# Moving one transpose per sequence from behind the scores to the end of the step before, and the first keys' copy to ScalarE, in a one-layer language-model kernel

## The reference

```python
h = layernorm(word_emb[x] + pos_emb + type_emb[mask]) * gamma + beta
a = layernorm(h)
k, q, v = a @ Wk, a @ Wq, a @ Wv              # split into 16 heads of 16
k, q = layernorm(k) * kln_w + kln_b, layernorm(q) * qln_w + qln_b   # per head
attn = softmax(causal(q @ k.T / 4))
h = h + (attn @ v) @ Wo + bo
n = layernorm(h)
scores = softmax(n @ gate_w.T);  top 2 of scores + expert_bias
h = h + sum over the two of  (silu(s*n @ w1[e]) * (s*n @ w3[e])) @ w2[e]    # s: the token's score
```

## Time and profile before

| | |
|---|---|
| Median of 3 runs | 545.32 us (545.27 to 545.44) |
| The profiled execution's own time | 545.62 us |
| Its span, first to last instruction | 543.8 us |
| Granted TensorE clock, mean | 0.992 |
| Start, 0 to 31.2 us (before the first scores): PE / DVE / ACT / POOL busy | 21.2 / 16.3 / 3.9 / 18.1 us |
| Scores of step 0 to scores of step 14, 31.2 to 186.2 us | 141.2 / 136.4 / 131.3 / 111.3 us of 155.0 |
| Last steps and routing, 186.2 to 228.8 us | 36.3 / 34.3 / 19.9 / 22.4 us of 42.6 |
| Experts, 228.8 to 543.8 us | 302.6 / 104.9 / 95.7 / 134.4 us of 315.0 |

### The profile page before, as it was taken

One profiled execution on the slowest core, in us unless ns is written; L12 is line 12 of the kernel. 1 busy time (PEld: TensorE's weight loads), 2 busy tenths in 40 slices (PEclk: granted clock), 3 DMA queues, 4 the chain that ended last, 5 costly groups with the idle time before them and its releaser, 6 DMA issues.

```text
span 543.8 us, 13452 instructions
## 1 busy us (share of the span) xinstructions
PE 501.2 (92%) x4470; PEld 428.7 (79%) x4471; DVE 291.9 (54%) x759; ACT 250.7 (46%) x575; POOL 286.2 (53%) x532
## 2 busy tenths in 40 slices
PE   5877989998999888999999999999999999999991
PEld 2345666777776665499999999999999999999980
DVE  2778888889989887733333333333333333333330
ACT  1166788978997883243223322332233323332320
POOL 4678787677764675214543454345434454344432
PEclk9999999999999999999999999999999999999996
DMA  5007721101028672302212221122112221222221
GB/s 174 10 22 243 231 85 31 58 29 29 29 80 278 212 251 84 90 22 41 29 30 39 39 39 22 37 39 39 23 36 39 39 28 31 39 38 30 30 39 19
DMA packets 29962, 36.75 MB, mean 68 GB/s; under 512 B 8272, under 2 KB 23504, under 8 KB 29936
## 3 DMA queue, kind: packets, MB, share of 16 engines
q0 software_dynamic: 8352, 12.76, 13.8%
q1 hardware_dynamic: 20768, 22.61, 13.1%
q10 hardware_dynamic: 816, 1.06, 0.6%
HBM read 26.81 MB, written 9.50 MB: 67 GB/s over the span
## 4 chain that ended last, share of the span: by engine, by line
PE 79%; DVE 5%; POOL 5%; ACT 4%; issue 3%; DMA 2%; POOLq 0%; DVEq 0%; ACTq 0%
PE PS L1445 35%; PE PS L1456 18%; PE PS L1172 10%; PE PS L1296 5%; PE PS L1254 2%; PE PS L1395 2%; PE PS L1271 2%; DMA x_pair<-word_dram,idx 1%; PE PS L1180 1%; ACT work L628 1%; PE PS L1310 1%; PE PS L1243 1%; DVE nmax L879 1%; DMA out_dram<-x_pair,dst_c 1%; POOL arena L477 1%
## 5 line engine op out<-in xcount | busy, mean ns | idle before, releaser
L1445 PEld LDWEIGHTS PS<-work,arena 128*128 128x128 f32 x1716 | 197.6, 192 | 2.3 <-ACT work L744 0.4
L1445 PE MATMUL PS<-work,arena 128*128 128x128 f32 x1716 | 198.0, 275 | 0.0
L750 ACT ACTIVATE work<-PS 128x768 f32<-128x768 f32 x39 | 31.6, 810 | 197.2 <-PE PS L1445 197.2
L1456 PE MATMUL PS<-w_sb,work 128*128 x468 | 107.6, 379 | 0.7 <-DVE x_pair L1147 0.7
L1139 DVE TENSOR_TENSOR work<-work,PS 128x640 f32<-128x640 f32 x39 | 32.0, 821 | 138.0 <-ACT work L750 138.0
L1456 PEld LDWEIGHTS PS<-w_sb,work 128*128 128x128 f32 x468 | 85.9, 190 | 11.2 <-issue 1.1
L572 POOL DMA_INDIRECT out_dram<-x_pair,dst_c x39 | 79.2, 2030 | 21.9 <-POOL dst_c L571 20.5
L571 POOL COPY dst_c<-dest_i 128x1 int32 (+1 forms) x39 | 7.1, 183 | 138.7 <-DVE x_pair L1147 136.5
L628 ACT ACTIVATE work<-PS,nmax 128x128 f32<-128x128 f32 x256 | 72.0, 401 | 3.7 <-DVE nmax L879 3.7
L740 ACT ACTIVATE arena<-w_sb 128x1408 f32 x40 | 55.1, 1379 | 12.0 <-DVE er_i L1115 9.0
L1172 PE MATMUL PS<-ident,work 128*128 128x128 f32 x336 | 54.8, 276 | 1.8 <-ACT work L628 1.8
(11 more groups left out here) (172 smaller groups left out, 618.8 us busy)
## 6 DMA issues: line engine op xcount, KB each, us to landing
w_sb<-w_dram SPq DMA_DIRECT2D x16, 640.0 KB, 5.6
w_sb<-w_dram SPq DMA_DIRECT2D x8, 704.0 KB, 4.5
x_rows<-x SPq DMA_DIRECT2D x16, 128.0 KB, 2.3
out_dram<-arena SPq DMA_DIRECT2D x16, 128.0 KB, 2.4
w_sb<-w_dram SPq DMA_DIRECT2D x16, 64.0 KB, 6.2
w_sb<-w_qkv_dram ACTq DMA_DIRECT2D x1, 768.0 KB, 8.2
work<-x_rows,src_c POOLq DMA_INDIRECT x41, 2.8
out_dram<-x_pair,dst_c POOLq DMA_INDIRECT x39
```

Of the source, the lines that this page charges most:

```text
L1445: last = n.matmul(up_ps[p][:, i, c, :], ws[p][:, k, at:at + P], xT_sb[p][:, k, :], start=(k == 0), stop=(k == DK - 1))
L1456: last = n.matmul(PS[:, 7, 0:D], hT_sb[p][:, i, :], w2_sb[:, bass.ds(e, 1), i, :], start=(i == 0), stop=(i == FK - 1))
```

## The change

Three things are edited.

- `early_rows(u)` is true for the sequences 0 to 3. For these the transposes of `a_n` stay where they were. For sequences 4 to 15 they move from step u-2, behind the scores, to the end of step u-3, behind `mask_banks`, and go to the upper half of `VY_BANK`; they wait for `a_ready`, `aT_ready` and `v_ready`. ScalarE's copy moves likewise, from the head of its step to the end of the step before.
- `outputs` waits for `aT_ready` only in step 1; from step 2 on it waits for `var_f` instead. `rank(0)`, which uses the same half of `VY_BANK`, gets a wait for the last `aT_ready`.
- The keys of sequences 0, 1 and 2 are copied out by ScalarE, at the head of `queries_out`, which for these waits for the transposes (`qk_ps`) and not for `k_ready`; the three `keys_out` calls on VectorE go. In step 0 `queries_out(1)` moves ahead of `transposed(2)`.

```diff
+        KEYS_BY_ACT = 3
+        def early_rows(u):
+            return isinstance(u, int) and u < 4
...
                 def queries_out(u):
-                    act.wait_ge(k_ready, u + 1)
+                    if isinstance(u, int) and u < KEYS_BY_ACT:
+                        act.wait_ge(qk_ps, u + 1)
+                    else:
+                        act.wait_ge(k_ready, u + 1)
                     if not isinstance(u, int) or u > 0:
                         act.wait_ge(s_done, RG * u)
+                    if isinstance(u, int) and u < KEYS_BY_ACT:
+                        a.activation(kT.rearrange("p b s -> p (b s)"), PS[:, T_BANK, D:2 * D], ACT.Identity,
+                                     scale=cols_sb[:, 4:5], bias=cols_sb[:, 5:6]).then_inc(k_ready, 1)
...
                 u = t + 2
-                if valid(u):
+                if valid(u) and early_rows(u):
                     act.wait_ge(aT_ps, u + 1)
                     wait(act, v_done, u - 1)
                     a.activation(aT[p].rearrange("p k s -> p (k s)"), PS[:, O_BANK, 0:D],
...
                     transposed(1)
+                    queries_out(1)
                     transposed(2)
-                    queries_out(1)
...
                 if valid(t):
                     transposed(3)
+                u = t + 3
+                if valid(u) and valid(t) and not early_rows(u):
+                    act.wait_ge(aT_ps, u + 1)
+                    act.wait_ge(v_done, u - 1)
+                    a.activation(aT[1 - p].rearrange("p k s -> p (k s)"), PS[:, VY_BANK, D:2 * D],
+                                 ACT.Copy).then_inc(aT_ready, 1)
...
                     normalize_a(2)
-                    keys_out(0)
...
                     first_norm(3)
-                    keys_out(1)
...
                     first_norm(4)
-                    keys_out(2)
...
                     pe.wait_ge(v_ready, B - 2)
+                    pe.wait_ge(aT_ready, B)
...
                     pe.wait_ge(v_ready, u + 1)
-                    wait(pe, aT_ready, u + 4)
+                    if at_step(t, 1):
+                        pe.wait_ge(aT_ready, u + 4)
                     if at_step(t, B):
                         pe.wait_ge(added, 1)
-                    elif edge and t + 2 >= B:
+                    else:
                         wait(pe, var_f, u)
...
                 u = t + 2
-                if valid(u):
+                if valid(u) and early_rows(u):
                     pe.wait_ge(a_ready, u + 1)
-                    wait(pe, var_f, u - 3)
                     wait(pe, aT_ready, u)
                     transposes(a_n, DK, O_BANK).then_inc(aT_ps, 1)
...
                 if valid(t + 1) and valid(t):
                     mask_banks(t + 1)
+                u = t + 3
+                if valid(u) and not early_rows(u):
+                    pe.wait_ge(a_ready, u + 1)
+                    pe.wait_ge(aT_ready, u)
+                    pe.wait_ge(v_ready, u - 1)
+                    transposes(a_n, DK, VY_BANK, D).then_inc(aT_ps, 1)
```

## The result

The changed kernel takes 547.12 us (median of 8 runs, 546.73 to 550.44), the kernel before in the same measurements 545.50 (8 runs, 545.27 to 546.01). The ratio is 1.0038, 95% interval 1.0022 to 1.0055: slower by 0.4%, 1.6 us. The forecast was slower by 1.25 us, 546.6.

The account below looks back on a forecast made before the run. TensorE, busy 501.2 of 543.8 us, was taken as the bound. Keys -1.85, moved pairs +4.18 and outputs -1.08 sum to +1.25 us on the 545.32 median: 546.6 us, range 544.3 to 548.4.

Parts of the forecast that it names:

- The wait moves to the qkn transposes: Steps 2 to 13: TensorE's wait before the outputs reappears before the qkn transposes; steps 4 to 13 gain only 1.08 us.
- Pairs of transposes in the solid row, 0.38 each: Ends of steps 1 to 12: each moved transpose pair costs TensorE 0.38 us before the next scores, 11 x 0.38 = +4.18.
- One pair free behind step 2: End of step 2: the moved pair costs nothing, as TensorE waits 0.82 us at step 3's x2 transposes anyway.
- The keys part, -1.85: Steps -1 to 1: key copies on ScalarE start squared sums, maxima and GpSimd's chain 1.85 us earlier; bounds 1.0 and 2.1.
- B: Moved pairs cost 0.22 us each, overlapped with the mask banks: sum -0.51, 544.8 us, no difference; chance 0.15.
- C: The 0.60 us wait is really saved in 12 steps, as VectorE's chain to qkn shortens: 536.1 us; chance 0.08.
- D: Step ends: the moved pair waits for v_ready or at the loop's branch, 0.12 us more per step: 548.0; chance 0.12.
- E: Start: the keys on ScalarE bring nothing, GpSimd's chain or ScalarE takes the gain back, +3.1: 548.4 us; chance 0.05.

## Why the prediction was right, and where its terms were off

- **The wait moves to the qkn transposes**: shown, by the idle time (1.00 in step 9, none before L1286 in steps 2 to 12) and by the run with normalize_qk between the maxima, in which that wait follows it. The gain per step was mis-sized: I had 3.11 us from scores to qkn in odd steps by step 14's release of 0.06. In steps 5, 7 and 9 it is 3.18 to 3.19, TensorE starts 0.13 us behind normalize_qk's end, and nothing is won: it started 0.13 behind it in the kernel before already, so the transposes stood at this release even then. In even steps it is 3.13, as forecast.
- **Pairs of transposes in the solid row, 0.38 each**: 0.36 where neighbours are 32-row groups, but 0.20 to 0.29 at the three turns of the loop. The direction of the two errors is opposite, and steps 4 to 13 came out at +2.11 for +2.34. The doubled pair puts the changes of shape at 0.14 in all, where I had read 0.1 for each. The Trainium skill's rule that a change of tiling mode drains TensorE (TensorEngine Tiling (Array Packing), section Tiling Modes) agrees in direction with 0.36 against 0.22; no run isolates the drain.
- **One pair free behind step 2**: half right. TensorE waits 0.72 us at x2 in step 3, was 0.82, so only 0.1 went into the wait. From the scores of step 2 to these transposes it is 0.14 us longer, for the forecast's 0, and from there to the scores of step 4 0.26, for 0.38. The sum, +0.40 for +0.38, is near because the two errors cancel.
- **The keys part, -1.85**: 1.81. Squared sums came at 29.55 us (forecast 29.86) and the maxima at 30.76 (30.9), of which 0.28 is the early projection. From this projection to the scores of step 1 it is 14.21 to 14.25 us in the three profiled kernels without the keys part, 12.40 in the changed kernel and 12.23 to 12.24 in the other eight with it: 1.8 to 2.0 us.
- **What was missing**: the granted clock. I had taken 1.00 for step 1 because it was 1.00 in the one profile that I had. In the changed kernel 0.85 us go there. Why it fell is open: TensorE's idle times are as they were, and the run with VectorE's statistics moved has the same list and the same idle times in step 1 (0.57, 0.56 and 1.45 us) and kept 1.00. The result of +1.60 is the forecast's 1.25 with these 0.85 on top, 0.28 off before the change begins, and 0.2 off in the steps. So the nearness of the number is in part luck. With the clock held the same change came to +0.7 us, so the forecast's own terms are about 0.5 too high.
- **The rivals**: B (cheap pairs) falls with the timeline, though at the loop's turns the price is B's. C (the intended gain) falls with it too: normalize_qk ends 3.05 us after the scores' start, as before. D's place was wrong: the pair waits for nothing, and ahead of the loop's branch it is cheaper, not dearer. E falls with the keys part alone.
- The sentence that let me discard C was "VectorE starts with the scores' end and works without a gap". It was truer than I used it: the same list also holds x2, which was already as late as TensorE, and ScalarE's list was 0.14 us from the same point. That is why the reordering, from which I expected 6 us, gave nothing.

## What to carry to other kernels

A wait in a pipelined step says which chain ended last, not by how much: before pricing its removal, read when the input of the instruction behind it was ready. Here that was 0.13 us before it started, and behind it stood two more lists within 0.2. Work moved out of a place with idle time into one without costs its full price even though TensorE has no instruction more. Moving it into the new wait was cheaper by 1.9 us, but not moving it at all was better still by 0.6. The gain that stayed was at the start, where the engines wait in a chain and nothing runs beside it.

## What the runs showed of the hardware

- The granted clock of TensorE fell to its lower level for some 3 to 7 us in steps 0 and 1, in some profiled executions and not in others: in step 1 in four of the five kernels with the keys part and without warm matmuls, and once from 30 to 36 us, over instructions that ran at the upper level in the kernel before. The fifth kernel, in which TensorE has the same instructions and idle times in step 1, kept the upper level. With five matmuls in the idle time in front it was 1.00 in all four kernels that had them.
- A pair of 128 x 128 transposes costs TensorE 0.22 us beside its like, 0.36 between groups of 32-row matmuls, and 0.20 to 0.29 at the loop's turn, which by itself takes 0.24 to 0.29.
- With normalize_qk 0.6 us earlier, TensorE's step was no shorter (11.10 us for 11.11 in step 9, 11.25 for 11.07 in step 8): the lists of three engines, in a loop over one another's results, end within 0.2 us of one another there.
- In the odd steps of the loop VectorE's instruction for x2, beside GpSimd's gather, took 0.59 to 0.69 us and ended 0.08 to 0.09 after the gather, or took 0.41 as elsewhere.
